# A gated cross-attention and expert kernel: the indirect writes of its last batches laid between other work on GpSimd

## What is computed

```python
logits = xf @ Wg + bg
idx = jnp.argmax(softmax(logits), axis=-1)
h = gelu(einsum('th,ehi->tei', xf, W1) + b1)
y = einsum('tei,eih->teh', h, W2) + b2
out = take_along_axis(y, idx[:, None, None], axis=1)[:, 0, :]
```

## Time and profile before

| | |
|---|---|
| time, median of 3 runs | 300.7 us (300.69 to 301.26) |
| profiled execution | 300.25 us, span 298.4 us |
| busy, share of the span | PE 94%, PEld 73%, DVE 70%, POOL 44%, ACT 35% |
| chain that ended last | PE 75%, DVE 8%, SPq 5%, issue 3%, DMA 2%, POOL 2% |
| line 1262, writes to `routed_rows` | x32, 32.5 us, mean 1016 ns |
| line 1300, stores | x39, 38.3 us, means 986 and 979 ns |
| mean granted clock of TensorE | 0.988 |

### The profile page before, as it was taken

How to read it: one execution, slowest core, us unless ns; L and a number is a source line. 1 busy time by engine, 2 the same in 40 slices (tenths; PEclk the granted TensorE clock), 3 DMA queues, 4 the chain that set the end, 5 groups by cost and what they waited for, 6 DMA issues and landing times.

```text
span 298.4 us, 9824 instructions
## 1 busy us (share of the span) xinstructions
PE 279.1 (94%) x3181; PEld 216.9 (73%) x3182; DVE 209.5 (70%) x611; ACT 105.3 (35%) x258; POOL 130.3 (44%) x157
## 2 busy tenths in 40 slices
PE   7989999999999999999999999968788999999970
PEld 6558677677776776767767777857677999999960
DVE  6576586696785875978668678867588766666650
ACT  2021321303213113032130320355555777877730
POOL 9512041243624525336154352722757555445551
PEclk9999999999999999999999999999999999999995
DMA  7666255464674746637646643423334544344210
GB/s 264 197 196 162 67 141 146 122 218 139 194 194 132 221 128 210 216 96 218 189 146 208 178 130 107 123 73 90 110 113 152 162 142 131 97 133 117 85 56 0
DMA packets 30955, 43.25 MB, mean 145 GB/s; under 512 B 7629, under 2 KB 17998, under 8 KB 30928
## 3 DMA queue, kind: packets, MB, share of 16 engines
q1 hardware_dynamic: 17872, 21.48, 25.9%
q10 hardware_dynamic: 9648, 12.86, 14.3%
q0 software_dynamic: 3408, 8.59, 8.2%
HBM read 24.83 MB, written 10.60 MB: 119 GB/s over the span
## 4 chain that ended last, share of the span: by engine, by line
PE 75%; DVE 8%; SPq 5%; issue 3%; DMA 2%; POOL 2%; ACT 1%; DVEq 1%; ACTq 1%; POOLq 0%
PE ps_pr L397 17%; PE ps_qo L405 16%; PE ps_so L430 8%; PE ps_av L451 8%; PE ps_tr L599 5%; PE ps_av L611 4%; PE ps_so L599 4%; PE ps_to L611 4%; PE ps_tr L439 3%; PE ps_pr L587 2%; PE ps_to L464 2%; SPq L318 2%; SPq L326 2%; DMA sb_wkv<-wkv_in 2%; ACTq L318 1%
## 5 line engine op out<-in xcount | busy, mean ns | idle before, releaser
L397 PE MATMUL ps_pr<-sb_wkv,sb_ct 128*128 128x512 f32 x128 | 62.1, 609 | 0.8 <-DMA sb_wkv<-wkv_in 0.5
L659 ACT ACTIVATE sb_pe_x<-sb_pe_x 128x512 f32<-128x512 f32 x16 | 10.1, 631 | 112.0 <-DVE sb_pe_x L817 112.0
L1247 POOL TENSOR_SCALAR sb_ve<-sb_mv 128x2 f32<-128x2 f32 x16 | 3.5, 220 | 88.1 <-DVE sb_mv L786 84.5
L397 PEld LDWEIGHTS ps_pr<-sb_wkv,sb_ct 128*128 128x128 f32 x128 | 22.5, 189 | 20.5 <-issue 19.9
L802 DVE STREAM_TRANSPOSE sb_y_q<-sb_q_n 128x512 f32<-128x512 f32 x16 | 17.4, 1090 | 26.8 <-ACT sb_q_n L654 26.8
L1262 POOL DMA_INDIRECT routed_rows<-sb_xs,sb_pos_i x32 | 32.5, 1016 | 8.3 <-issue 7.7
L405 PE MATMUL ps_qo<-sb_wog,sb_ot 128*128 128x264 f32 x128 | 31.4, 388 | 1.1 <-ACT sb_ot L670 1.1
L405 PEld LDWEIGHTS ps_qo<-sb_wog,sb_ot 128*128 128x128 f32 x128 | 24.1, 190 | 11.2 <-issue 6.2
L430 PE MATMUL ps_so<-sb_kb,sb_y_q 128*32 128x128 f32 x1024 | 31.0, 273 | 0.5 <-DVE sb_y_q L802 0.5
L451 PE MATMUL ps_av<-sb_vb,sb_at 128*32 128x128 f32 x1024 | 31.3, 274 | 0.0
L451 PEld LDWEIGHTS ps_av<-sb_vb,sb_at 128*32 128x32 f32 x1024 | 27.0, 110 | 5.0 <-issue 5.0
(11 more groups left out here) (143 smaller groups left out, 481.4 us busy)
## 6 DMA issues: line engine op xcount, KB each, us to landing
sb_kb<-sb_y_k SPq DMA_DIRECT2D x124, 32.0 KB
sb_vb<-sb_y_v SPq DMA_DIRECT2D x124, 32.0 KB
sb_ct<-ctx_in ACTq DMA_DIRECT2D x15, 256.0 KB, 3.0
sb_x<-x_in ACTq DMA_DIRECT2D x15, 256.0 KB, 3.5
sb_xt<-xt_in_ ACTq DMA_DIRECT2D x14, 256.0 KB, 5.1
sb_xb<-routed_rows SPq DMA_DIRECT2D x25, 134.0 KB, 2.1
sb_w_all<-w_in_ SPq DMA_DIRECT2D x4, 514.0 KB
sb_w<-w_in SPq DMA_DIRECT2D x4, 512.0 KB
```

Source lines behind the costliest of these rows:

```text
L397: last = pe.matmul(pr[:, s * 512:(s + 1) * 512], lhsT=ct[i][:, kc, s, :], rhs=wkv[:, kc, :], start=(kc == 0), stop=(kc == KC - 1))
L659: act.activation(pe_x[:], pe_x[:], ACT.Exp, scale=float(H) ** -0.5).then_inc(exp_done, 1)
```

## The change

Four edits. The division of pair 14 goes from GpSimd to VectorE, right behind `turn_o` of that pair. Of the four writes of batch 6, the first stands before the power of pair 15, the second behind it, the third and fourth behind stores 0 and 1. The four writes of batch 7 stand behind stores 3, 5, 7 and 9, where all four had stood behind store 2. The last batch gets four columns of row numbers of its own in `pos_i`, and `place_3` no longer waits for earlier writes for it, since its numbers no longer overwrite those of batch 6.

```diff
--- before.py
+++ after.py
@@ -154,7 +154,7 @@
         base = sb("base", [P, E])
         rb = sb("rb", [P, 4, E])
         pos = sb("pos", [P, 4])
-        pos_i = sb("pos_i", [P, 4], U32)
+        pos_i = sb("pos_i", [P, 8], U32)
         pad_row = sb("pad_row", [P, ROW])
         nbm = sb("nbm", [P, E, 32])
         nb = sb("nb", [P, E])
@@ -203,6 +203,11 @@
         def rows_of(j):
 
             return xs[j // 2][:, 2 * (j % 2):2 * (j % 2) + 2, :]
+
+        def row_numbers(m):
+
+            first = 4 if isinstance(m, int) and m == last_batch else 0
+            return pos_i[:, first:first + 4]
 
         def rank_ps(m, first, end):
 
@@ -918,8 +923,9 @@
 
             def place_3(m):
                 dve.wait_ge(pos_step, 2 * m + 2)
-                wait(dve, routed, 64 * m)
-                dve.tensor_copy(pos_i[:], pos[:]).then_inc(pos_done, 1)
+                if not isinstance(m, int) or m < last_batch:
+                    wait(dve, routed, 64 * m)
+                dve.tensor_copy(row_numbers(m), pos[:]).then_inc(pos_done, 1)
 
             b_num, b_rows = cst[:, C_BLK:C_BLK + 1], cst[:, C_BLK + 1:C_BLK + 2]
 
@@ -1111,6 +1117,7 @@
                 tab_9(0)
                 tab_10(0)
                 turn_o(n)
+                divide(dve, n)
                 stats_1(n - 1, (n - 1) % 4)
                 stats_2(n - 1, (n - 1) % 4)
                 largest(n + 1)
@@ -1255,12 +1262,23 @@
                 pool.wait_ge(res_var, n + 1)
                 pool.tensor_tensor(rows_of(j)[:, :, RSTD], ve1[:], neg_half[:], ALU.pow).then_inc(res_pow, 1)
 
+            def route_tile(j, s, batch):
+
+                c = 2 * (j % 2) + s
+                pool.indirect_dma_start(rows, bass.IndirectOffsetOnAxis(ap=row_numbers(batch)[:, c:c + 1], axis=0),
+                                        rows_of(j)[:, s, :], None).then_inc(routed, 16)
+
             def route(j, batch):
 
                 wait_apart(pool, pos_done, batch + 1, passed_pool)
                 for s in range(2):
-                    pool.indirect_dma_start(rows, bass.IndirectOffsetOnAxis(ap=pos_i[:, 2 * (j % 2) + s:2 * (j % 2) + s + 1], axis=0),
-                                            rows_of(j)[:, s, :], None).then_inc(routed, 16)
+                    route_tile(j, s, batch)
+
+            def route_nth(batch, i):
+
+                if i == 0:
+                    wait_apart(pool, pos_done, batch + 1, passed_pool)
+                route_tile(2 * (batch % 2) + i // 2, i % 2, batch)
 
             def slot(k, c, t):
                 if has(k, -1):
@@ -1278,12 +1296,11 @@
                 for j in range(2):
                     route(2 * ((m - 1) % 2) + j, m - 1)
                 pow_x1(n - 2, (n - 2) % 4)
-                divide(pool, n)
                 pow_x1(n - 1, (n - 1) % 4)
                 pow_x1(n, n % 4)
-                for j in range(2):
-                    route(2 * (m % 2) + j, m)
+                route_nth(m, 0)
                 pow_x1(n + 1, (n + 1) % 4)
+                route_nth(m, 1)
 
             def pre():
                 pool.memset(vb[0][:].rearrange("p t f -> p (t f)"), 0.0).then_inc(vb_clear[0], 1)
@@ -1304,9 +1321,10 @@
             slots(pool, pre, slot, end, first=4, last=4, step=4)
             for b in range(EARLY):
                 store(b, b % RING, b // RING)
-                if b == 2:
-                    for q in range(2):
-                        route(2 * (last_batch % 2) + q, last_batch)
+                if b < 2:
+                    route_nth(last_batch - 1, 2 + b)
+                elif b in (3, 5, 7, 9):
+                    route_nth(last_batch, (b - 3) // 2)
             block_slots(pool, store, 0)
```

## The result

Over 20 runs the changed kernel took 303.29 us in the median (its lowest 301.17) and the kernel before 300.69 us (299.53 to 301.94). The ratio is 1.0078, with a 95% interval of 1.0061 to 1.0094: slower by 0.8%, 2.3 us by the ratio and 2.6 by the medians. One of the 20 executions took 584 us and is not in the ratio. The profiled execution has a span of 301.9 us against 298.4. The forecast was 301.1 us and the range 300.2 to 302.7, so the median lies 0.6 us above its end.

What follows compares the result with a forecast made beforehand. The prediction took TensorE, wholly busy from 230 us, as the bound, so only its earlier idle time counted. Its terms 0 - 2.01 + 2.45 = +0.44 us on the 300.7 us median gave 301.1 us, range 300.2 to 302.7.

Steps and rivals of the forecast that it cites:

- The division: Pair 14's division moved to VectorE: its 0.69 us hidden by the wait for the fetch, cost and gain 0.
- The power: Pair 15's power on GpSimd, behind one write instead of four, starts earlier and lets pick_1 start 2.01 us sooner.
- The stall: TensorE before block 16's transposes: one new idle time of 2.45 us, as fetch 16 waits for the last write.
- The chain from the finish of block 5 to block 16's transposes: GpSimd's stores and writes, then SyncE, fetch and normalisation: from 225.48, block 16's transposes start at 241.03.
- the landing of the last write: Batch 7's last write, ending at 236.31 on GpSimd, lands 1.02 us later, at 237.33.
- an estimate of 2.3 us by the Trainium skill: One indirect write from issue to landing; would make the sum +0.8 instead of +0.4; the row's 1.98 us was kept.
- GpSimd's pace: Stores 5 to 9 and three writes on GpSimd: 7.78 us of work plus seven gaps totalling 2.17 us.
- the clock, the third: Rival: TensorE's clock falls in the stall at block 16; net +2.4 us, 303.1, half of it 302.1; chance 0.18.
- the second: Rival: each link of the chain to block 16 a little later; net +0.8 to +1.9 us, about 301.8; chance 0.20.
- The first, that the gain stays: Rival: the last write in GpSimd's queue is not held by the backlog; net -1.1 us, 299.6; chance 0.12.
- the reason given for the dropped wait of place_3: VectorE's place_3: dropping the wait costs nothing, since all of batches 0 to 5 had landed by then.

Runs made afterwards that it cites:

- e3: The kernel before with one edit, pair 14's division on VectorE; 300.45 us, ratio 0.9995 against the kernel before.
- e8: The changed kernel with batch 7's writes behind store 2 and pair 14's division back on GpSimd; 298.46 us, ratio 0.9905 against the kernel before.
- e2: The kernel before with one edit, batch 7's four writes behind stores 3, 5, 7 and 9; 305.76 us, ratio 1.0183 against the kernel before.
- e4: The changed kernel plus 12 unused matmuls on TensorE ahead of block 16's transposes; 301.53 us, ratio 1.0030 against the kernel before.
- e6: The changed kernel with the last write behind store 8 instead of store 9; 300.21 us, ratio 0.9983 against the kernel before.
- e10: The changed kernel run again on another chip; the changed kernel is 0.7 to 0.8% slower than the kernel before on these chips.
- e14: The changed kernel run again on a further chip; the changed kernel is 0.7 to 0.8% slower than the kernel before on these chips.
- e1: The changed kernel with batch 7's four writes back behind store 2; 297.91 us, ratio 0.9916 against the kernel before.
- e5: The changed kernel with batch 7's writes one each behind stores 2, 3, 4 and 5; 297.49 us, ratio 0.9879 against the kernel before.
- e7: The changed kernel with batch 7's writes behind store 2, row numbers shared again and place_3 waiting; 301.64 us, ratio 1.0025 against the kernel before.

## Why the prediction was wrong

Up to the idle time at block 16 the mechanism was the one forecast, link by link. The division: nothing (e3, e8). The power: pick_1 moved by 2.01 us by the forecast; with the fetch's 0.53 taken off, the profile has 214.16 + 0.53 - 212.66 = 2.03, and the ranks moved by 2.02. The stall: at block 16, once, released by the normalisation behind the fetch behind the last write. The chain from the finish of block 5 to block 16's transposes, by its terms:

```text
                                            forecast   changed kernel
finish of block 5 to store 5                0.88       0.88  (225.84 to 226.72)
store 5 to the end of the last write        9.95       10.28 (to 237.00)
end of the write to SyncE's release         1.02       1.63  (to 238.63)
SyncE to its fetch                          1.10       1.12  (to 239.75)
landing of the fetch                        2.10       2.10
normalisation and handovers                 0.50       0.50  (to 242.35)
sum                                         15.55      16.51
```

**The term that was mis-sized** is the landing of the last write. The forecast read it off the traffic: the write that ended at 209.13 moved no data after 210.2. But in the changed kernel the engine that waits is let go some time after the last data have moved. Its slices of 0.2 us show the difference:

```profile
237.80:238.00 0.20, 0.20 (x5) 0.20 (x4) 0.00 (x0) 0.00 (x0) 0.20 (x1) 1.00 0.57 215
238.00:238.20 0.20, 0.20 (x3) 0.19 (x2) 0.00 (x0) 0.00 (x0) 0.20 (x1) 1.00 0.07 22
238.20:238.40 0.20, 0.20 (x2) 0.19 (x1) 0.00 (x0) 0.15 (x1) 0.08 (x1) 1.00 0.00 0
```

The last traffic lies before 238.2, 1.2 us after the write's end, and SyncE goes on at 238.63. From the start of the write it is 2.71 us here, 2.51 in e2, 2.93 in e4, 2.76 in e6, where the forecast had 0.96 + 1.02 = 1.98. The forecast weighed an estimate of 2.3 us by the Trainium skill (DMA: Bandwidth & Descriptors, the section on the anatomy of one DMA on the GpSimd path) and kept the row's number; all four measured values lie above both, and the estimate is the nearer one. In e10 and e14, on the other chips, this row of the chain has 2.31 and 2.45 us. The other 0.33 us is GpSimd's pace: its indirect DMAs in this stretch took up to 1.07 us, not 0.98.

**The step that took the time out of the range** is the clock, a rival with a chance of 0.18. The forecast had the row that speaks for it (0.52, 2.1 us after the last matmul) and a stall of 2.45 us above that, and yet gave it less than one in five and left it out of the sum. With the stall of 3.3 us the fall costs 1.71 us in the profiled execution, and over the medians e4 takes 1.4 us back by filling it: its 301.53 us, the forecast's stall with a whole clock, lie within the range. The reason given against it, that TensorE is busy right before and right behind the stall, did not keep the clock up in the changed kernel and in e6 (2.09 us idle); in e2's profile, with 2.81 us, it stayed up. Without the fall the net would have been about 3.49 - 2.26 = +1.2 us; with it it is +2.9, against +2.3 by the ratio and +2.6 by the medians.

Of the rivals, the second (each link a little later, +0.8 to +1.9) and the third came true together, and they had been priced one at a time. The first, that the gain stays, is what e1 and e5 show for another place of the writes. Also wrong, though without effect on the forecast, was the reason given for the dropped wait of place_3, that batches 0 to 5 had landed by then. For the last batch the wait asks for batch 6 as well, and with the writes of batch 6 moved behind stores it would have been 3.5 us long (e7).

Two versions beat both kernels and are not told apart: e1's, the changed kernel with batch 7's four writes behind store 2, and e5's, with them behind stores 2 to 5. Only e5's was run on the other two chips, where it was faster too.

## What to carry to other kernels

When work is moved back in a queue because it seems to have time, look for the strictest waiter of the last piece, and add up the whole chain behind it: the queue's pace, the transfer's report, the waiter's own loop, the next transfer. Take the time of a transfer from a row in which somebody waited for it, not from its traffic. And if the sum gives TensorE an idle time in a stretch where it is the bound, count the slower work after it as part of the price when it is as long as those behind which the clock fell here (2.1 us in e6; 1.6 with two shorter ones behind it in e3), and look whether a later idle time gives it back.

## What the runs showed of the hardware

- An indirect write of 128 rows held its waiter for 2.3 to 2.9 us from the start of the instruction where no fetch was issued beside it, and for 4.35 us in e7, where one was issued at 216.90. The traffic was over before the waiter went on: 0.4 us in the changed kernel. In e7 the bulk of what moved was over by 220.4, and a trickle of 20 GB/s until 221.2 was the end.
- The granted clock fell to half behind an idle time of 2.1 us in one execution (e6) and stayed whole behind 2.8 us in another (e2). Behind 3.3 us in the changed kernel it fell, was at half from 243.1 to 246.5, and cost 1.7 us. It also fell behind 1.6 us followed by two idle times of about 0.5 us (e2, e3), and stayed whole behind the same ones in the kernel before.
- Behind such a fall e3 lost 0.1 us and the changed kernel 1.7 us: in e3 a later idle time shrank by it.
- The same kernel before took 300.6 to 300.8 us on two chips and 307.9 and 308.2 us on two others, where ScalarE and VectorE stood 3.5 us and more in waits without a known releaser in the profiles taken there, of other kernels.
